# Second layer of a two-layer sequence model: GpSimd's scatters and returns, each made to wait until the one before has landed

## The reference

```
logits = xf @ Wr.T + br
expert_idx = argmax(logits, axis=-1)                       # 1 of 8 experts for each token
h = relu(einsum('td,efd->etf', xf, W1) + b1[:, None, :])   # 128 -> 512
y = einsum('etf,edf->etd', h, W2) + b2[:, None, :]         # 512 -> 128
out = y[expert_idx, arange(tokens)]
x = layernorm(x + out)
```

## Time and profile before

| what | value |
|---|---|
| median of three timed executions | 1368.16 us (1364.99 to 1369.56) |
| span of the profiled execution | 1397.4 us |
| busy in that span: PE, DVE, POOL, ACT | 91%, 79%, 73%, 68% |
| second group's 16 scatters, first to last issue | 1268.45 to 1288.94 us |
| the 46 returns, first to last issue | 1290.20 to 1379.71 us |

### The profile page before, as it was taken

The page is one execution under the profiler, slowest core; times in us unless marked ns, Lnnn a source line. Parts: engine busy times, 40 slices in busy tenths (PEclk is TensorE's granted clock), DMA queues, the critical chain, the costliest instruction groups (busy, mean ns, idle before and its releaser), DMA issues.

```text
span 1397.4 us, 27753 instructions
## 1 busy us (share of the span) xinstructions
PE 1272.1 (91%) x9894; PEld 962.1 (69%) x9894; DVE 1097.7 (79%) x1829; ACT 947.2 (68%) x1630; POOL 1013.4 (73%) x620
## 2 busy tenths in 40 slices
PE   6799999999999999999998779999989999986695
PEld 2567767676777676766766646689966666656693
DVE  5799999999999999999999953333357888874475
ACT  5888988898889888988988842245545555532243
POOL 2789999999999999999999916223334665664442
PEclk9999999999999999999999999999999999998798
DMA  5545434543444454444444351312152000021223
GB/s 187 145 131 161 138 139 118 161 149 129 139 139 165 133 150 139 164 132 152 139 146 111 114 216 47 90 44 86 56 157 86 2 1 1 13 64 34 79 72 100
DMA packets 153014, 154.73 MB, mean 111 GB/s; under 512 B 96624, under 2 KB 121712, under 8 KB 143168
## 3 DMA queue, kind: packets, MB, share of 16 engines
q1 hardware_dynamic: 148112, 143.16, 32.8%
q0 software_dynamic: 4768, 9.81, 2.2%
HBM read 138.66 MB, written 20.20 MB: 114 GB/s over the span
## 4 chain that ended last, share of the span: by engine, by line
PE 49%; ACT 21%; DVE 16%; issue 8%; another core or an unknown queue 2%; DMA 2%; POOL 1%; SPq 1%; DVEq 1%; POOLq 0%; ACTq 0%
DVE hh L887 7%; PE pq L410 6%; ACT da L720 6%; PE pa L506 4%; PE py L525 3%; ACT pa L725 3%; PE bank L1562 3%; PE bank L1558 2%; PE pr L2016 2%; PE bank L1572 2%; PE pr L2219 2%; PE pr L2030 2%; PE bank L1478 2%; DVE hh L897 2%
## 5 line engine op out<-in xcount | busy, mean ns | idle before, releaser
L1042 POOL TENSOR_TENSOR hc<-hh,cs 128x1024 f32<-128x1024 f32 x256 | 596.9, 2369 | 24.6 <-DVE hh L887 21.7
L887 DVE TENSOR_TENSOR_SCAN hh<-da,st,pa 128x512 f32<-128x512 f32 x240 | 292.7, 1261 | 14.1 <-PE pa L506 12.6
L525 PE MATMUL py<-ident,hc 128*128 128x128 f32 x2048 | 268.4, 277 | 7.4 <-ACT yt L738 5.8
L525 PEld LDWEIGHTS py<-ident,hc 128*128 128x128 f32 x2048 | 229.1, 141 | 54.4 <-issue 29.1
L506 PEld LDWEIGHTS pa<-dg,dtut 64*128 64x128 f32 x2560 | 160.9, 189 | 107.0 <-issue 103.2
L506 PE MATMUL pa<-dg,dtut 64*128 64x128 f32 x2560 | 189.8, 285 | 29.6 <-DVE hh L887 20.6
L720 ACT ACTIVATE da<-dt,w 128x512 f32<-128x512 f32 x320 | 209.7, 711 | 0.2
L897 DVE TENSOR_TENSOR_SCAN hh<-pa,st,hh 128x512 f32<-128x512 f32 x144 | 175.2, 1265 | 6.1 <-POOL hh L1032 3.7
L725 ACT ACTIVATE pa<-dt,w 128x512 f32<-128x512 f32 x192 | 124.5, 680 | 35.2 <-DVE hh L887 20.8
L410 PE MATMUL pq<-xn,w 128*128 128x512 f32 x248 | 124.6, 627 | 3.6 <-ACT xn L755 3.6
L1032 POOL TENSOR_TENSOR hh<-dtu,bs 128x1024 f32<-128x1024 f32 x48 | 112.8, 2365 | 3.1 <-issue 1.9
(11 more groups left out here) (341 smaller groups left out, 2643.8 us busy)
## 6 DMA issues: line engine op xcount, KB each, us to landing
cs<-bcrows SPq DMA_DIRECT2D x64, 1024.0 KB, 4.9
dg<-blocks SPq DMA_DIRECT2D x80, 256.0 KB, 5.0
bs<-bcrows SPq DMA_DIRECT2D x48, 256.0 KB, 3.7
blocks<-bcrows SPq DMA_DIRECT2D x320, 1.0 KB, 3.2
xsorted<-in_pads SPq DMA_DIRECT2D x13, 387.0 KB, 5.7
rot<-in_rot SPq DMA_DIRECT2D x4, 1024.0 KB, 4.9
wx<-in_l_w SPq DMA_DIRECT2D x4, 1024.0 KB, 10.0
ysort<-ytoken SPq DMA_DIRECT2D x14, 256.0 KB
```

Source lines behind the costliest of these rows:

```text
L525: i = pe.matmul(py[:, h * CH + kt * P:h * CH + (kt + 1) * P], hc[s % HCS][:, h, t], ident[:, :], is_transpose=True, start=n == 0 and kt == ...
L887: v.tensor_tensor_scan(hh[(NS * m + nj) % HHS][:, h, :], da[q % DAS][:, :], inflows, 0.0 if first else st[:, m % 2, nj, h:h + 1], ALU.mult ...
L1042: g.tensor_tensor(hc[s % HCS][:, :, :], hh[s % HHS][:, :, :], cs[j % 2][:, s % CG, :].unsqueeze(1).broadcast_to([P, HF, CH]), ALU.mult).th ...
```

## The change

The second group's scatters wait one by one: ahead of each but the first GpSimd waits until the scatter ahead of it has landed. The wait for eight at once goes. The scatters of the first group stay as they are. In the returns, each but the very first waits, besides for its own tile (`s_ys`), until the return ahead of it has landed; the first of the second group waits for the last of the first.

```
@@ -1966,8 +1966,8 @@
                     for i in tiles:
 
-                        if place and i and i % 8 == 0:
-                            g.wait_ge(s_scat1[place], scat0[place] + 16 * i)
+                        if place and i >= 1:
+                            g.wait_ge(s_scat1[place], scat0[place] + 16 * (i - 0))
                         t = i % B * TB + place * GC + i // B
                         g.indirect_dma_start(out=xsorted[1], out_offset=bass.IndirectOffsetOnAxis(ap=pos[:, place, i:i + 1], axis=0),
                                              in_=xn[:, t, :], in_offset=None).then_inc(s_scat1[place], 16)
@@ -2076,6 +2076,9 @@
                         g.wait_ge(s_token, j // SG + 2)
                     g.wait_ge(s_ys, J0 + j + 1)
+                    if j >= 1:
+                        before_place, before_j = (j - 1) // SG, (j - 1) % SG
+                        g.wait_ge(s_ret1[before_place], ret0[before_place] + 16 * (before_j + 1))
                     g.indirect_dma_start(out=ytoken, out_offset=bass.IndirectOffsetOnAxis(ap=token[:, j:j + 1], axis=0),
                                          in_=ysort[:, j, :], in_offset=None).then_inc(s_ret1[j // SG], 16)
```

## The result

The changed kernel takes 1473.11 us (median of 4 runs, 1465.23 to 1473.89), the kernel before 1368.86 us beside it (4 runs, 1364.99 to 1372.72): a ratio of 1.0749, interval 1.0712 to 1.0786. That is 104.3 us more. The forecast was 72.3 us more; 1473.11 lies above 1440.5 by 32.6 us and above the range's end, 1453. The direction and the place were right. The price of one link in the returns was not.

The account below looks back on a forecast made before the run. Tiles were taken to bound the kernel before, GpSimd's DMA queue the changed one: 60 periods of 2.6 us plus 18.95 replace 128.95 us, 46.0 more; with 26.3 of pauses, 1368.16 + 72.3 = 1440.5 us, range 1409 to 1453.

Parts of the forecast that it names:

- the period: Second group's scatters and returns: issue to next issue with a landing between, taken as 2.6 us, ends 2.23 and 3.15.
- each of the 60 DMAs carries its wait: Claim that 15 scatters and 45 returns each hold their new wait in the instruction stream, so the change takes effect.
- Rival 3: Scatters and returns: landings slow beside other work, 3.15 us in all 60 links; 1473.5 us, or 1447.2; chance 4%.
- From the profile's time to the metric: Step from profiled span to timed runs: cost 46.0 + 26.3 = 72.3 us, assuming timed runs lack the pauses.
- pauses: VectorE's four waits for "remote" between 1268 and 1308 us, 26.3 us in all, taken as absent from timed runs.
- rival 1: Tiles between 1268 and 1308 us: pauses in every execution, so cost is 46.0 us alone; 1414.2 us; chance 30%.
- rival 4: Stretch of dense issues: spacing the DMAs removes the pauses, tiles end up to 26.3 us earlier; 1341.9 us; chance 2%.
- So from there on the tiles set the pace, not GpSimd: Returns from 1308.74 us on in the kernel before: each waits for its tile, one every 1.89 us, 0.94 idle.
- 42.3 us of tile waits: GpSimd's waits for VectorE in 34 returns, to be swallowed by landing waits, so the price is 46.0, not 80.4 us.
- GpSimd is last: At tile 45: done about 1397.6 us, GpSimd comes at 1425.7, leaving 28 us of room.
- the stall of the tiles behind tile 33: VectorE at the first group's last norm stands still some 19 us, hidden behind the queue of returns.
- Rival 2: Scatters and returns: the wait hides descriptor preparation, 2.23 us per link; 1418.3 us, or 1392.0 with pauses; chance 6%.

Follow-up runs that it names:

- the returns alone: Kernel before with only the returns' landing waits added, the scatters still waiting for eight: 1453.09 us, ratio 1.062.
- the other order: Changed kernel with each return's landing wait written ahead of its tile wait: 1449.96 us, ratio 1.0594.
- the scatters' second wait: Changed kernel with one more wait, for a long-set semaphore, in each second-group scatter from the second on: 1477.07 us, ratio 1.0798.
- the repeated kernel: Kernel before, no line changed, profiled once more: 1368.6 us, ratio 1.0011.
- one wait in four: Changed kernel with landing waits only ahead of every fourth second-group scatter and every fourth return: 1388.08 us, ratio 1.0155.

## Why the prediction was wrong in size and right in kind

**The failed step** is the one on the period: "GpSimd then needs a moment from the landing to its next issue. The 0.30 us in which it waits for nothing between two issues is the nearest row for that". The landing was right: 2.21 to 2.24 us from issue to landing in 39 of the 46 returns, as in the earlier trace rows. By the Trainium skill ("DMA: Bandwidth & Descriptors", section "Anatomy of one DMA — SWDGE (gpsimd) path") it was 2.15 us, an estimate by that page; the measured landing agrees within 0.1 us. The moment was right for the scatters too: their landing's wait stands on the DMA, as in the nearest rows, and the shortest link is 2.54 us. A return had a wait already, for its tile. With a second one, the landing's goes to an instruction of its own ahead of the DMA, and the moment is 0.74 us. No row of before showed that kind of wait, and "each of the 60 DMAs carries its wait" held for the scatters alone. The order of the two waits in the returns and the second wait in the scatters moved the cost in both directions, by 0.48 and 0.45 us a link, so this is shown. It is 45 x (2.97 less 2.60) = 16.7 of the 27.8 us.

**The other 11.1 us of the returns** lie in eight longer links, which the forecast had none of: 9.0 us in seven late landings (2.40 to 5.34 us where 2.22 is normal) and 2.1 us in one late restart.

The two longest landings stand beside a load that SyncE has just started: issues at 1312.37 and 1385.66 with loads from 1310.61 and 1384.91, 3.1 and 1.9 us over the normal link. The first of them moved with its load in the returns alone (load at 1288.74, return at 1291.68) and stayed with it in the other order (load at 1311.55, return at 1313.02). That shows the coincidence; a run that moves the load and nothing else wasn't made.

Three more late landings, 3.4 us in all, have a packet of another queue in flight beside them, which the profile calls "instruction": the returns issued at 1321.43, 1334.84 and 1408.88 (the last has a store of SyncE beside it too). For the first of them the DMA view of its flight (1321.43 to 1325.2) has these lines (packets, MB and share by queue; then the return and its us to landing):

```profile
q0 software_dynamic: 32, 0.07, 5.6%
q8 instruction: 1, 0.02, 2.5%
...
ytoken<-rot,token POOLq DMA_INDIRECT x1, 3.8
```

The return just ahead, issued at 1318.45, has no such packet beside it and lands after 2.2 us. This too is a coincidence and not a shown cause: in the other order one such packet lies beside two scatters with normal landings.

The late restart is the link from 1341.92 to 1347.03: its landing is normal, and the next issue comes 2.89 us behind it. The same return, the eleventh, is late in the returns alone and with the scatters' second wait (5.11 us in both), and in the other order (3.7 us). So it belongs to this place in the program; why stays open.

Rival 3's 1473.5 is near the result mostly by accident: it put 3.15 us into each of the 60 periods, by slow landings. Slow landings there are, but they make 9.0 of the 27.8 us, and the restart, of which rival 3 says nothing, makes 16.7. GpSimd's issues themselves kept their length (median 957 ns, at most 1127), so they lengthened nothing.

**From the profile's time to the metric: right in direction, 4.3 us short.** I put the forecast 2.9 us under its span, by calling 26.3 of the 29.2 us pauses. An execution of this kernel takes 2.2 us more than its span (1473.89 against 1471.7), and the median lies 0.8 us under the profiled one: 1.4 us above the span. 28.3 and 4.3 make the 32.6 us by which the forecast was low. The pauses were indeed no part of the timed runs: the repeated kernel has none, and the span grew by 74.3 us while the times grew by 104.3, so rival 1 falls. What made them stays open. The dense issues, which rival 4 blames, are there in the repeated kernel as well, so they don't make them every time.

**"So from there on the tiles set the pace, not GpSimd"** was true of one disturbed execution only. The argument that the 42.3 us of tile waits would swallow part of 80.4 us hung on it. In a normal execution 6.5 us are there to be swallowed: 80.4 less 6.5 is 73.9, near 46.0 + 26.3 = 72.3, so both ways lead to one number; but the reason given was of the profile, not of the kernel, and one wait in four showed the difference.

**Right:** GpSimd is last, by 38 us (forecast 28); the stall of the tiles behind tile 33 comes (43.7 us where 19 were forecast, "longer where the pauses are missing") and costs nothing beside the queue of returns; the links of the scatters and of the returns reach from the first scatter to the tail without a break; start and tail came out within 1.1 and 0.2 us. The chain as the profile draws it leaves the landings twice for the tiles (1313 to 1344 and 1388 to 1399 us), since it puts some of GpSimd's waits down to a tile (15.0 us in six returns). The landings speak against that: 44 of the 45 links end 0.74 to 0.77 us behind the landing of the return ahead, and the late restart is the other one. Rival 2's bare 2.23 us falls: every link has idle time and a moment behind the landing.

## What to carry to other kernels

A queue of DMAs that each wait for the one ahead, as here on GpSimd, costs landing plus restart per link, and the restart has to be taken from an instruction that waits in the same form: see whether the DMA already carries a wait, and if it gets a second, write the one that comes last in time first (here 0.48 us a link, 45 times). And before a base is read for what "sets the pace", check that the profiled execution is a normal one: this one's span was 29.2 us over the median, and the waits for tiles that I read in it as slack were 42.3 us where a normal execution has 8.4.

## What the hardware showed that was not expected

- From landing to next issue: 0.27 us where the wait for the landing stands on the DMA (2.49 less 2.22, returns in the other order), 0.74 us where it stands on an instruction ahead of it (2.97 less 2.23).
- Landings of up to 5.3 us (5.5 in the returns alone) beside a load by another queue that has just started, where the normal one is 2.22 us.
- Landings of 3.0 to 3.8 us with a packet of the queue "instruction" in flight beside them; only the coincidence is shown.
- One restart of 2.89 us, at the same return in three runs.
- Four pauses with 26.3 us of VectorE's idle time in one profiled execution, and in none of the seven that followed.
